# Layer-3 attention: scores from two float32r parts in the two row halves of the array, denominators in spare value columns

## What is computed

```python
def _L3_xattn_ref(q, k, v, gamma):       # q = layernorm(x), k = v = ctx_2048, each (64, 64, 256)
    h = 8; dq = Dq // h                  # 8 heads of 8 positions each
    qh = q.reshape(B, h, dq, Lq)         # (64, 8, 8, 256)
    kh = k.reshape(B, h, dq, Lk)
    vh = v.reshape(B, h, dv, Lk)
    qk = jnp.einsum('bhdq,bhdl->bhql', qh, kh) * (1.0 / sqrt(dq))
    sm = jax.nn.softmax(qk, axis=-1)     # over the 256 features
    ret = jnp.einsum('bhql,bhdl->bhdq', sm, vh)
    return gamma * ret.reshape(B, Dv, Lq)
```

## Time and profile before

| | us |
|---|---|
| median of three runs | 2261.21 (2259.16 to 2265.93) |
| profiled execution, its own time | 2276.26 |
| its span | 2274.0 |
| granted TensorE clock, mean over the span | 0.924 |

### The profile page before, as it was taken

The page is one execution under the profiler, slowest core; times in us unless marked ns, Lnnn a source line. Parts: engine busy times, 40 slices in busy tenths (PEclk is TensorE's granted clock), DMA queues, the critical chain, the costliest instruction groups (busy, mean ns, idle before and its releaser), DMA issues. The chain is left out here.

```text
span 2274.0 us, 46815 instructions
## 1 busy us (share of the span) xinstructions
PE 1915.3 (84%) x15870; PEld 1457.1 (64%) x15870; DVE 1592.3 (70%) x3825; ACT 995.0 (44%) x2486; POOL 1115.9 (49%) x1467
## 2 busy tenths in 40 slices
PE   6979845398885988898887897899999998879993
PEld 5869612387664777777776787466666664547772
DVE  7865732469668889898886665888888785443446
ACT  3733221134233455554443332466666665423330
POOL 4630026524365666666663100488888775643331
...
GB/s 211 230 102 54 10 117 175 186 20 6 63 128 26 1 0 0 0 0 0 0 0 11 69 39 1 31 109 109 109 108 109 106 86 88 88 94 96 106 108 238
DMA packets 140384, 172.62 MB, mean 76 GB/s; under 512 B 31410, under 2 KB 121698, under 8 KB 135586
## 3 DMA queue, kind: packets, MB, share of 16 engines
...
...
## 5 line engine op out<-in xcount | busy, mean ns | idle before, releaser
L2855 DVE TENSOR_REDUCE mx<-bank 128x2 f32<-128x512 f32 x512 | 321.0, 678 | 77.9 <-PE bank L2722 77.2
L2825 ACT ACTIVATE e<-bank 128x512 f32<-128x512 f32 x512 | 269.1, 606 | 135.3 <-PE bank L2742 135.3
L2668 POOL TENSOR_TENSOR es<-e 128x256 f32<-128x256 f32 x384 | 271.7, 730 | 90.5 <-ACT e L2825 90.0
L1915 POOL TENSOR_TENSOR q_l<-q_l,rot_l 64x512 f32<-64x512 f32 x128 | 162.3, 1268 | 131.0 <-DVE rot_l L2113 131.0
L2722 PE MATMUL bank<-k,q 72*128 72x256 bf16 x1024 | 203.6, 284 | 15.7 <-DMA k<-k_parts 7.5
L2742 PE MATMUL bank<-q,k 74*128 74x256 bf16 x1024 | 195.5, 274 | 5.9 <-DMA q<-rows 3.8
L2759 PE MATMUL bank<-e,val 128*32 128x256 f32 x2048 | 138.8, 388 | 3.1 <-ACT nd L2820 0.7
L2722 PEld LDWEIGHTS bank<-k,q 72*128 72x128 bf16 x1024 | 92.0, 100 | 76.5 <-issue 24.5
...
L1947 PE MATMUL bank<-qcT,wq_abs 96*128 96x128 f32 x1024 | 127.4, 285 | 0.0
L1947 PEld LDWEIGHTS bank<-qcT,wq_abs 96*128 96x128 f32 x1024 | 121.5, 198 | 2.5
L1972 PE MATMUL bank<-wvo,rd_l 128*128 128x256 f32 x512 | 116.4, 381 | 0.0
...
...
## 6 DMA issues: line engine op xcount, KB each, us to landing
...
```

The costliest lines, as they stand in the source:

```text
L1915: nc.gpsimd.tensor_tensor(q[64:P, j, four(m), :], q[64:P, j, four(m), :], rot[64:P, j, four(m), :], ALU.add).then_inc(s["rope_added"], 1)
L2668: nc.gpsimd.tensor_tensor(es[:, n, :], e[:, n, 0, :], e[:, n, 1, :], ALU.add).then_inc(s["sum_ready"], 1)
L2825: nc.scalar.activation(e[:, slot(i, r), :, :].rearrange("p k n -> p (k n)"), scoresT(r)[:, :], ACT.Exp).then_inc(s["exp_ready"], 1)
L2855: v.tensor_reduce(mx[:, a.n, 0, at:at + 2], scores(r)[:, :].rearrange("p (a n) -> p a n", a=2), AX.X, ALU.max, negate=True).then_inc(s["ma ...
```

## The change

- **Two parts instead of three.** Normalized x and ctx are split in two float32r parts (a rounded one and the rest), and the four products are stacked: `ROWS3` = 32 rows a head. A first row beyond them (row 32: ones in `k`, zero in `q`) and two for the maximum follow, 33 rows in `score_pair` and 35 in `turned_pair`. The weights and the moving operand are float32r, so also 4 bytes wide in memory.
- **Two heads in the array's two row halves.** Units r = 0 and 2 lie in partitions 0 and up, r = 1 and 3 in 64 and up (`BASE3`, `place`). The matmuls of a pair are issued alternately.
- **TensorE's order** in a quad becomes: turned pair 0 (r = 0, 1), score pair 0, score pair 1, `read` of the quad before, turned pair 1 (r = 2, 3). `turned_bank` and `turned_after` stay.
- **Denominators.** The stationary operand of the values has 32 columns of which 8 were used in a quad. Now 8 spare ones are ones, so the same matmul sums `e`. Quads 0 and 1 collect in the left half of bank 6, quads 2 and 3 in the right. `add_lengths` and the matmuls against ones go. The numerators of one half then lie in other partitions than their denominators: `merge` on SP moves both to `merged` with 16 DMAs a tile, 16 partitions by 1 KB each, ahead of `lay_rows` in SP's order. `invert` waits for them and stands behind unit (3, 1) instead of (2, 0).
- **DMAs.** Per tile SP issues two stores instead of three (`store`), four loads of `q` instead of one, four of `k` instead of three, two of the maxima's rows instead of one. The stages before are changed to suit: two parts in layer 0, and four settings of fixed rows instead of one for each of eight steps in the ternary stage.

```diff
-BUF3, ROWS3 = 4, 9 * DQ3
+BUF3, ROWS3 = 4, 4 * DQ3
+BASE3, TOP_ROW3 = (0, P // 2), ROWS3 + 1
...
             def split(t):
-                parts, rest, src = k_parts[:, t % KR, :, :], k_rest[:, t % KR, :], ctx_in[:, t % CTX, :]
+                parts, src = k_parts[:, t % KR, :, :], ctx_in[:, t % CTX, :]
                 pool.wait_ge(s[ctx_loaded[t % CTX]], 32 * (t // CTX) + 32)
-                wait(pool, k_stored[t % KR], 48 * (t // KR))
-                nc.gpsimd.tensor_copy(parts[:, 0, :], upper(src))
-                nc.gpsimd.tensor_tensor(rest, src, upper(src), ALU.subtract).then_inc(s["a_split"], 1)
+                wait(pool, k_stored[t % KR], 32 * (t // KR))
+                nc.gpsimd.tensor_copy(parts[:, 0, :], src).then_inc(s["a_split"], 1)
                 pool.wait_ge(s["a_split"], t + 1)
-                nc.gpsimd.tensor_copy(parts[:, 1, :], upper(rest))
-                nc.gpsimd.tensor_tensor(parts[:, 2, :], rest, upper(rest), ALU.subtract).then_inc(s["k_low_ready"], 1)
+                nc.gpsimd.tensor_tensor(parts[:, 1, :], src, whole(parts[:, 0, :]), ALU.subtract).then_inc(s["k_low_ready"], 1)
 
...
+            def fixed_rows(t):
+
+                for n, (a, value) in enumerate(((c.k3, 1.0), (c.q3, 0.0))):
+                    for m, base in enumerate(BASE3):
+                        at = slice(base + ROWS3, base + 2 * ROWS3)
+                        nc.gpsimd.memset(whole(a[at, t, :]), value).then_inc(s["p_keys"], 1)
+                        pool.wait_ge(s["p_keys"], 4 * t + 2 * n + m + 1)
...
+def head_rows(ap, both, g):
+
+    return ap[:, :, 2 * H3 * both:2 * H3 * both + 2 * H3, :].rearrange("a c (b g h) l -> g (a c) b (h l)", b=2, g=2)[g]
+
+
+def copied_rows(ap, both, g, b):
+
+    return head_rows(ap, both, g)[:, b, :].unsqueeze(1).broadcast_to([2 * DQ3, 2, H3 // 2 * D])
...
             def store(a):
-                wait(sp, "mid_ready", a.t + 1)
-                settle(sp, s["sp_passed"])
                 wait(sp, "low_ready", a.t + 1)
                 settle(sp, s["sp_passed"])
-                for n in range(3):
+                for n in range(2):
                     sp.dma_start(c.q_parts[n, :, bass.ds(a.t * 2 * H3, 2 * H3), :].rearrange("c h l -> h c l"),
-                                 parts[:, a.n % 2, n, :]).then_inc(s[stored[a.n % 2]], 16)
+                                 whole(parts[:, a.n % 2, n, :])).then_inc(s[stored[a.n % 2]], 16)
 
             def load(a):
-                sp.wait_ge(s[stored[a.n % 2]], 48 * (uses(a) + 1))
+                sp.wait_ge(s[stored[a.n % 2]], 32 * (uses(a) + 1))
                 settle(sp, s["sp_passed"])
-                cols, both = bass.ds(2 * a.t * H3, 2 * H3), slice(2 * a.n, 2 * a.n + 2)
-                q_rows = c.q_parts[:, :, cols, :].rearrange("a c h l -> (a c) (h l)").unsqueeze(1)
-                sp.dma_start(q[0:R, both, :], q_rows.broadcast_to([3 * DQ3, 3, 2 * H3 * D])).then_inc(s[qk_loaded[a.n]], 16)
-                k_rows = c.k_parts[:, :, cols, :].rearrange("c m h l -> (c m) (h l)")
-                for m in range(3):
-                    sp.dma_start(k[3 * DQ3 * m:3 * DQ3 * (m + 1), both, :], k_rows).then_inc(s[qk_loaded[a.n]], 16)
+                both = slice(2 * a.n, 2 * a.n + 2)
+                for g, base in enumerate(BASE3):
+                    for b in range(2):
+                        sp.dma_start(whole(q[base:base + R, 2 * a.n + b, :]),
+                                     copied_rows(c.q_parts, a.t, g, b)).then_inc(s[qk_loaded[a.n]], 16)
+                    for m in range(2):
+                        sp.dma_start(whole(k[base + 2 * DQ3 * m:base + 2 * DQ3 * (m + 1), both, :]),
+                                     head_rows(c.k_parts, a.t, g)).then_inc(s[qk_loaded[a.n]], 16)
...
-                sp.dma_start(q[R:R + 2, 2 * a.n:2 * a.n + 2, :], rows[:, a.n, :]).then_inc(s[rows_loaded[a.n]], 16)
+                for g, base in enumerate(BASE3):
+                    at = slice(base + TOP_ROW3, base + TOP_ROW3 + 2)
+                    sp.dma_start(whole(q[at, 2 * a.n:2 * a.n + 2, :]),
+                                 whole(rows[4 * H3 * g:4 * H3 * g + 4 * H3, a.n, :])).then_inc(s[rows_loaded[a.n]], 16)
+
+            def merge(a):
+
+                b = a.n % 2
+                sp.wait_ge(s["out_copied"], tile_ready(a.t))
+                sp.wait_ge(s["x_done"], tile_ready(a.t) - 2)
+                settle(sp, s["sp_passed"])
+                for r in range(4):
+                    low, high = slice(32 * r, 32 * r + 16), slice(32 * r + 16, 32 * r + 32)
+                    for dst, part, src, half_at in ((low, 0, low, 0), (high, 0, high, 1), (low, 1, high, 0), (high, 1, low, 1)):
+                        sp.dma_start(merged[dst, b, part, :], nd[src, b, half_at, :]).then_inc(s[all_merged[b]], 16)
 
             def tile(a):
+                if a.exists(-1):
+                    merge(a.to(-1))
...
+                        if (i, r) == (3, 0) and a.exists(AHEAD):
+                            x_low(a.to(AHEAD))
+                        if (i, r) == (3, 3) and a.exists(-1):
                             finish(a.to(-1))
-                        if (i, r) == (3, 0) and a.exists(AHEAD):
-                            rest_and_low(a.to(AHEAD))
...
-            def score(a, i, r, turned=None):
-                if i == 0 and r == 0:
-                    pe.wait_ge(s[qk_loaded[a.n]], 64 * a.g + 64)
-                pe.wait_ge(s["max_ready"], unit_ready(a.t, i, r) - NP1)
+            def score_pair(a, i, p, turned=None):
+                if i == 0 and p == 0:
+                    pe.wait_ge(s[qk_loaded[a.n]], 128 * a.g + 128)
+                pe.wait_ge(s["max_ready"], unit_ready(a.t, i, 2 * p + 1) - NP1)
                 if turned is not None:
                     pe.wait_ge(s["rows_ready"], tile_ready(turned.t))
-                b, h = batch_head(a.n, i, r)
                 for qt in range(2):
-                    last = nc.tensor.matmul(scores(r)[:, qt * D:(qt + 1) * D],
-                                            q[0:R, b, h * D + qt * P:h * D + qt * P + P],
-                                            k[0:R, b, h * D:(h + 1) * D], start=True, stop=True)
-                last.then_inc(s["scores_ready"], 1)
+                    for r in (2 * p, 2 * p + 1):
+                        base, b, at = place(a.n, i, r)
+                        last = nc.tensor.matmul(scores(r)[:, qt * D:(qt + 1) * D],
+                                                q[base:base + R + 1, b, at + qt * P:at + qt * P + P],
+                                                k[base:base + R + 1, b, at:at + D], start=True, stop=True)
+                        if qt == 1:
+                            last.then_inc(s["scores_ready"], 1)
...
-            def score_turned(a, i, r):
-                if i == 0 and r == 0:
-                    pe.wait_ge(s[rows_loaded[a.n]], 16 * a.g + 16)
-                pe.wait_ge(s["exp_ready"], unit_ready(a.t, i, r) - turned_after[r])
-                b, h = batch_head(a.n, i, r)
+            def turned_pair(a, i, p):
+                if i == 0 and p == 0:
+                    pe.wait_ge(s[rows_loaded[a.n]], 32 * a.g + 32)
+                pe.wait_ge(s["exp_ready"], max(unit_ready(a.t, i, r) - turned_after[r] for r in (2 * p, 2 * p + 1)))
                 for lt in range(DK):
-                    last = nc.tensor.matmul(scoresT(r)[:, lt * D:(lt + 1) * D],
-                                            k[:, b, h * D + lt * P:h * D + lt * P + P],
-                                            q[:, b, h * D:(h + 1) * D], start=True, stop=True)
-                last.then_inc(s["turned_ready"], 1)
+                    for r in (2 * p, 2 * p + 1):
+                        base, b, at = place(a.n, i, r)
+                        used = slice(base, base + TOP_ROW3 + 2)
+                        last = nc.tensor.matmul(scoresT(r)[:, lt * D:(lt + 1) * D], k[used, b, at + lt * P:at + lt * P + P],
+                                                q[used, b, at:at + D], start=True, stop=True)
+                        if lt == DK - 1:
+                            last.then_inc(s["turned_ready"], 1)
...
-                if i in SUMMED:
-                    pe.wait_ge(s["sum_ready"], 4 * (len(SUMMED) * a.t + i + 1) + 16)
-                else:
-                    pe.wait_ge(s["exp_ready"], unit_ready(a.t, i, 3))
+                pe.wait_ge(s["exp_ready"], unit_ready(a.t, i, 3))
                 if i == 0:
                     pe.wait_ge(s["val_ready"], tile_ready(a.t))
                     pe.wait_ge(s["out_copied"], tile_ready(a.t) - 1)
+                side = slice(i // 2 * D, i // 2 * D + D)
                 for lt in range(DK):
                     for r in range(4):
-                        nc.tensor.matmul(readout[32 * r:32 * r + 32, 0:D], val[:, a.n % 2, r, i, lt, :],
-                                         e[:, slot(i, r), lt, :], start=(i == 0 and lt == 0),
```

(30 more changed lines are left out.)

190 lines of the change are left out of this document (79 added, 111 removed).

## The result

The changed kernel takes 2521.33 us (median of four runs, 2518.12 to 2526.36) against 2261.59 (2259.16 to 2265.93) for the kernel before, measured beside it: ratio 1.1148, 95% interval 1.1123 to 1.1173. The forecast was 2403 and its range ended at 2500. The kernel is slower, as forecast, but by 260 us instead of 142.

A forecast was written before the change was run, and what follows sets the result against it. TensorE was taken to bound the kernel before at 14.13 us a tile. At 18.4, 30 tiles add 128 us, the last two tiles 6, the last merge 8: +142 on 2261.2 gives 2403, range 2300 to 2500.

The forecast's parts named there:

- The clock: Layer-3 attention: granted clock at 1.00 and 0.50 for about half the tiles each, 15.5 and 21.3 averaging 18.4 us a tile.
- the start from the prologue's 0.50: Layer-3 attention: the steady loop starts from the prologue's granted clock of 0.50, a reason to expect a lower clock.
- Rival 3: Layer-3 attention: halves run together, clock 0.50 throughout, 21.3 us a tile, 2496 us; chance 0.12.
- The full-clock tile of 15.5: Layer-3 attention at full clock: 13.65 us from the quads, plus 0.9 for quad 0's read and 1.0 for DVE.
- The chain of 3.41 a quad: TensorE-ACT loop, closing once a quad: matmuls, read, turned pair 1, two exponentials; 3.41 us a quad, 13.65 a tile.
- a merge issue: SP's 16 merge DMAs a tile: 0.37 us an issue as for plain rows, 5.9 in all, just covered.
- SP's own round: SP's DMA work a tile, merge, rows, stores and their landing, loads: 13.6 to 16.5 us, nearly the bound too.
- Rival 4: Merge issues on SP at 0.59 us: 19.0 us a tile at full clock, 2418 us; chance 0.05.
- The last merge: End of the attention: the last tile's merge has no cover, 5.9 + 2.0 = 7.9, 8 us once.
- The last two tiles: End of the attention: equal at full clock, 1.5 us a quad longer at the lower one, half of 12: +6 us.
- rival 2: Score matmuls: weight loads of the halves queue, a pair costs 0.24 us, 17.2 a tile, 2363 us; chance 0.22.
- Rival 5: Layer-3 attention: ACT's loop does not bind, TensorE's relief reaches DVE, 11.9 us a tile, 2203 us; chance 0.04.

The follow-up runs named there:

- 33-row fillers: Changed kernel with eight unread matmuls a quad over 33 rows added behind turned pair 1: 2544.3 us, beside 2263.8 for the kernel before.
- the spread version: Row halves, old denominators, turned pair 1 ahead of the read, rotated banks, reciprocal in two separated halves, later transpose, against the kernel before: 2261.93 us beside 2275.77, ratio 0.9933.
- the run with full fillers: Changed kernel with eight unread matmuls a quad over all 128 rows added behind turned pair 1: 2580.5 us, beside 2282.5 for the kernel before.
- the longer read: Changed kernel and order, but denominators as in the kernel before (POOL sums, matmuls against ones, no merge): 2538.8 us, beside 2280.5 for the kernel before.
- the run in which SP bound: Changed kernel with turned pair 1 moved ahead of the value read, merges kept: 2470.3 us, beside 2263.8 for the kernel before.
- longer reads: Four of eight read matmuls issued twice: without merges and with turned pair 1 ahead 2282.0 us (before 2280.5); in the changed kernel 2592.8 (before 2284.0).

## Why the prediction was wrong

**The clock, the step that failed.** "I expect it at either level for about half the tiles" and so 18.4 us a tile. It was 0.50 in all of them. Of the 118 us by which the forecast fell short, 112 are these tiles (240 for 128) and 11 the end (25 for 14); some 5 us elsewhere go the other way. I weighed only rests and the start from the prologue's 0.50. The runs show that the rows in use weigh as well: busy 98 us of 100 with 33-row fillers the clock stays at 0.50, and as many fillers over 128 rows raise it to 0.70 to 0.80. The start does not hold it down: the spread version begins at 0.50 too (1440 to 1460 us) and is at 1.00 from 1480 on. Rival 3 was the right case. Its 21.3 us a tile was mis-sized by 1.2: two of the quads took 5.40 for my 5.19 (to the read 1.58 for 1.42, the read 1.87 for 1.96, turned pair 0.83 for 0.67), quad 3 took 5.51, and the read of quad 0 waited 0.65 for 0.5.

**The full-clock tile of 15.5, the step behind it.** The chain of 3.41 a quad holds nearly: with the changed kernel's own read a quad takes 3.61 in the run with full fillers (1620.07 to 1623.68, ended by an exponential), with the longer read 4.20 for 4.07. But a merge issue costs 0.59 to 0.63 us, not 0.37: I took the price of the plain rows, and it is that of the rearranged ones. The range "13.6 to 16.5" for SP's own round is 20.06 us in the run in which SP bound. SP's issues don't go by TensorE's clock (0.63 us in that run at 0.50, 0.68 with full fillers at full clock), so a tile could hardly have come under 20 us while the merges stood on SP; in the run with full fillers they made TensorE wait 5.3 us in a tile. Rival 4 had the mechanism and gave it 0.05. At 0.50 the long tile hides all this, which is why it does not show in the changed kernel but at its end.

**The end.** The last merge was to cost 7.9 and took 12.5: its 16 issues alone are 10.00, and the reciprocal starts 11.4 after the copy ends. The last two tiles were to cost 6 as half of 12, and cost 12.5 since the clock was low in both.

**What held.** The order makes a loop through ACT, "nothing like 11.9": the order alone costs the kernel before 165 us. The halves run together in the main, and rival 2 falls. But a pair does not cost 0.12: four matmuls take 0.34 at full clock (1605.19 to 1605.53 with the changed order and old denominators), 0.17 a pair, and rival 2 had 0.24. The Trainium skill, "TensorEngine Tiling (Array Packing)", Key Properties, says that tiles can load weights and multiply in parallel, and the trace agrees. POOL and layers 0 to 2 cost nothing. The read of values alone takes 1.00 us at full clock up to the next turned pair (run with full fillers, 1624.59 to 1625.59); I had 1.01.

**Rival 5** said that TensorE's relief is worth something where no loop through ACT binds. In the changed order one does. With turned pair 1 ahead of the read, the old denominators, rotated banks and a spread reciprocal a tile is 13.81, under 14.44; I had found no such way. The 11.9 of the rival it does not reach.

Left open: in the changed kernel itself the rests and the narrow matmuls can't be parted, since taking away the rests leaves 0.50; only with longer reads do the rests show, 0.94 without them and 0.59 with them.
